# Expert stage: down projection of the odd experts as three products of split operands, five steps behind

## The reference

```
h = jnp.einsum('th,ehd->etd', xn, w1) + b1[:, None, :]
a = jnp.minimum(h[..., ::2], LIMIT)
b = jnp.clip(h[..., 1::2], -LIMIT, LIMIT)
s = a * jax.nn.sigmoid(ALPHA * a) * (b + 1.0)
y = jnp.einsum('eti,eih->eth', s, w2) + b2[:, None, :]
t = jnp.einsum('eth,te->th', y, gate_full)
return x + t.reshape(shape)
```

## Time and profile before

| | us |
|---|---|
| median of three runs | 1690.46 (1688.75, 1690.46, 1696.88) |
| the profiled execution | 1688.07 |
| its span, first to last instruction | 1686.30 |
| expert stage, first to last product of TensorE | 260.9 to about 867 |
| TensorE busy in the whole span | 1355.0 |
| VectorE busy in the whole span | 1255.6 |
| ScalarE busy in the whole span | 802.1 |

### The profile page before, as it was taken

One profiled execution on the slowest core, in us unless ns is written; L12 is line 12 of the kernel. 1 busy time (PEld: TensorE's weight loads), 2 busy tenths in 40 slices (PEclk: granted clock), 3 DMA queues, 4 the chain that ended last, 5 costly groups with the idle time before them and its releaser, 6 DMA issues. The chain is left out here.

```text
span 1686.3 us, 36641 instructions
## 1 busy us (share of the span) xinstructions
PE 1355.0 (80%) x13255; PEld 956.7 (57%) x13255; DVE 1255.6 (74%) x2799; ACT 802.1 (48%) x1432; POOL 145.7 (9%) x72
## 2 busy tenths in 40 slices
PE   0569998999999999999968888633777767678876
PEld 0456775666666666666636666432444544466665
DVE  6785127777777777777768999728888784799996
ACT  0564326666666666666646555311212211566663
POOL 2000000000000000000002443410000000112221
PEclk9879999999999999999989999867999999788887
DMA  8000003433334334333312433460223000111110
GB/s 226 1 0 0 6 5 103 116 114 114 113 113 112 108 113 113 113 113 114 113 42 75 125 112 126 129 236 24 78 106 124 31 29 32 54 57 56 56 56 19
DMA packets 122258, 142.22 MB, mean 84 GB/s; under 512 B 8768, under 2 KB 78752, under 8 KB 121120
## 3 DMA queue, kind: packets, MB, share of 16 engines
q1 hardware_dynamic: 118704, 134.81, 26.0%
q10 hardware_dynamic: 3440, 5.79, 1.0%
HBM read 106.49 MB, written 34.08 MB: 83 GB/s over the span
## 5 line engine op out<-in xcount | busy, mean ns | idle before, releaser
L919 ACT ACTIVATE glu_a<-moe_a,b1s 128x512 f32<-128x512 f32 x256 | 176.2, 688 | 227.8 <-PE moe_a L848 227.8
L865 PE MATMUL moe_y<-glu_a,w2s 128*128 128x512 f32 x512 | 261.3, 592 | 0.3 <-DVE glu_a L966 0.2
L949 DVE TENSOR_SCALAR b_raw<-b_raw 128x512 f32<-128x512 f32 x256 | 109.4, 427 | 146.9 <-ACT b_raw L924 146.6
L846 PE MATMUL moe_a<-x_hi,w_hi 128*128 128x512 f32 x256 | 192.5, 752 | 5.4 <-DVE w_lo L975 5.4
L924 ACT ACTIVATE b_raw<-moe_b,b1s 128x512 f32<-128x512 f32 x256 | 176.0, 687 | 2.6 <-PE moe_b L848 0.9
L966 DVE TENSOR_TENSOR glu_a<-glu_a,gate_row 128x512 f32<-128x512 f32 x256 | 175.8, 687 | 0.0
L958 DVE SCALAR_TENSOR_TENSOR glu_a<-glu_a,b_raw 128x512 f32<-128x512 f32 x256 | 175.6, 686 | 0.1
L865 PEld LDWEIGHTS moe_y<-glu_a,w2s 128*128 128x128 f32 x512 | 96.2, 188 | 23.9 <-DVE glu_a L966 2.0
L848 PE MATMUL moe_b<-x_hi,w_lo 128*128 128x512 f32 x256 | 101.9, 398 | 0.0
L848 PE MATMUL moe_a<-x_hi,w_lo 128*128 128x512 f32 x256 | 101.9, 398 | 0.0
L846 PE MATMUL moe_b<-x_hi,w_hi 128*128 128x512 f32 x256 | 101.9, 398 | 0.0
(11 more groups left out here) (252 smaller groups left out, 2791.8 us busy)
## 6 DMA issues: line engine op xcount, KB each, us to landing
gate_row<-gate_scratch SPq DMA_DIRECT2D x256, 256.0 KB, 3.1
kq_scratch<-kq_out SPq DMA_DIRECT2D x32, 256.0 KB, 3.5
kq_in<-kq_scratch SPq DMA_DIRECT2D x8, 1024.0 KB, 7.1
acc<-in_L_attn_inputs SPq DMA_DIRECT2D x8, 512.0 KB, 10.0
xq_scratch<-qT SPq DMA_DIRECT2D x16, 256.0 KB, 2.0
v_scratch<-v_out SPq DMA_DIRECT2D x16, 256.0 KB, 2.3
k_scratch<-k_out SPq DMA_DIRECT2D x16, 256.0 KB, 2.8
k_rows_scratch<-k_rows SPq DMA_DIRECT2D x16, 256.0 KB, 3.2
```

The source lines that it names most:

```text
L846: pe.matmul(bank[:, :], w1_hi[:, e, s, :], hi, start=True, stop=False)
L865: pe.matmul(bank, w["w2"][:, e, :], glu_a[e % 4][:, :], start=(e == 0), stop=(e == E - 1), skip_group_check=True).then_inc(down, 1)
L919: act.activation(glu_a[e % 4][:, :], ps_a[u][:, :], ACT.Gelu_apprx_sigmoid, bias=w["b1"][:, 0, e:e + 1]).then_inc(a_glu, 1)
L949: dve.tensor_scalar(b_raw[u][:, :], b_raw[u][:, :], 1.0 + LIMIT, 1.0 - LIMIT, ALU.min, ALU.max).then_inc(b_cut, 1)
```

## The change

For the eight odd experts, the fp32 down product is replaced by three one-pass products of split operands: w2 high x activation high, w2 high x activation low, w2 low x activation high. Four buffers of 128x512 hold the parts of the activation (`a_hi`, `a_lo`, two of each), two of 128x8x128 those of w2. The parts of w2 are made in the first tile, beside those of w1. The parts of the activation are made in even steps, of the weighed expert three steps back: the high one by ScalarE (a copy to fp32r, ahead of the gelu), the low one by VectorE (a subtraction, behind `multiply`). The odd experts' down products are five steps behind their up projection, in even steps; the even experts' stay one fp32 product, three steps behind, in odd steps. At the end the order is 11, 14, 13, 15. The gelu of an odd expert, which overwrites `glu_a`, waits for the low part of the expert four before it where it waited for that expert's product. `copy_y` waits for both counts.

```diff
--- before.py
+++ after.py
@@ -790,12 +790,23 @@
         ps_a = [ctx.enter_context(nc.psum_tensor(f"moe_a{i}", [P, TILE], F32)) for i in range(2)]
         ps_b = [ctx.enter_context(nc.psum_tensor(f"moe_b{i}", [P, TILE], F32)) for i in range(2)]
         ps_y = [ctx.enter_context(nc.psum_tensor(f"moe_y{i}", [P, SUBS, DIM], F32)) for i in range(2)]
+
+        w2_hi, w2_lo = sb("w2_hi", [P, EXPERTS // 2, DIM], F32R), sb("w2_lo", [P, EXPERTS // 2, DIM], F32R)
+        a_hi, a_lo = [sb(f"a_hi{i}", [P, TILE], F32R) for i in range(2)], [sb(f"a_lo{i}", [P, TILE], F32R) for i in range(2)]
+        w2_hi_ready, w2_lo_ready = sem("w2_hi_ready"), sem("w2_lo_ready")
+        a_hi_ready, a_lo_ready = sem("a_hi_ready"), sem("a_lo_ready")
+        down_split = sem("down_split")
         up_a, up_b, biased = sem("up_a"), sem("up_b"), sem("biased")
         b_copied, b_cut, a_glu = sem("b_copied"), sem("b_cut"), sem("a_glu")
         multiplied, weighted, down, added = sem("multiplied"), sem("weighted"), sem("down"), sem("moe_added")
         counted = sem("moe_counted")
         acc = w["acc"]
         E = EXPERTS
+        HALF = E // 2
+
+        def even_of(t, e):
+
+            return t * HALF + e // 2
 
         def before(t, e, k):
 
@@ -858,12 +869,23 @@
 
                 def down_proj(t, parity, e):
 
-                    pe.wait_ge(weighted, t * E + e + 1)
-                    if e == 0 and not (isinstance(t, int) and t < 2):
-                        pe.wait_ge(added, t - 1)
                     bank = ps_y[parity].rearrange("p j d -> p (j d)")
-                    pe.matmul(bank, w["w2"][:, e, :], glu_a[e % 4][:, :], start=(e == 0), stop=(e == E - 1),
-                              skip_group_check=True).then_inc(down, 1)
+                    if e % 2 == 0:
+                        pe.wait_ge(weighted, t * E + e + 1)
+                        if e == 0 and not (isinstance(t, int) and t < 2):
+                            pe.wait_ge(added, t - 1)
+                        pe.matmul(bank, w["w2"][:, e, :], glu_a[e % 4][:, :], start=(e == 0), stop=False,
+                                  skip_group_check=True).then_inc(down, 1)
+                        return
+                    i = e // 2
+                    if isinstance(t, int) and t == 0:
+                        pe.wait_ge(w2_lo_ready, i + 1)
+                    pe.wait_ge(a_lo_ready, even_of(t, e) + 1)
+                    hi, lo = a_hi[i % 2][:, :], a_lo[i % 2][:, :]
+                    pe.matmul(bank, w2_hi[:, i, :], hi, start=False, stop=False, skip_group_check=True)
+                    pe.matmul(bank, w2_hi[:, i, :], lo, start=False, stop=False, skip_group_check=True)
+                    pe.matmul(bank, w2_lo[:, i, :], hi, start=False, stop=(e == E - 1),
+                              skip_group_check=True).then_inc(down_split, 1)
 
                 def bias(t, parity):
 
@@ -880,16 +902,17 @@
 
                 def step(t, parity, e, more):
                     up(t, parity, e)
-                    if before(t, e, 3):
-                        tile, expert = before(t, e, 3)
-                        down_proj(tile, parity if e >= 3 else 1 - parity, expert)
+                    lag = 3 if e % 2 else 5
+                    if before(t, e, lag):
+                        tile, expert = before(t, e, lag)
+                        down_proj(tile, parity if e >= lag else 1 - parity, expert)
                     if e == 6 and not (isinstance(t, int) and t == 0):
                         turn_y(t - 1, 1 - parity)
                     if e == 9:
                         bias(t, parity)
 
                 def tail():
-                    for e in range(E - 3, E):
+                    for e in (E - 5, E - 2, E - 3, E - 1):
                         down_proj(TILES - 1, 1, e)
                     turn_y(TILES - 1, 1)
 
@@ -899,6 +922,16 @@
             def _(act):
                 def split(e):
                     act.activation(w1_hi[:, e, :, :], w["w1"][:, e, :, :], ACT.Copy).then_inc(w1_hi_ready, 1)
+                    if e % 2:
+                        act.activation(w2_hi[:, e // 2, :], w["w2"][:, e, :], ACT.Copy).then_inc(w2_hi_ready, 1)
+
+                def split_a(t, e):
+
+                    i, n = e // 2, even_of(t, e)
+                    act.wait_ge(weighted, t * E + e + 1)
+                    if before(t, e, 4):
+                        act.wait_ge(down_split, n - 1)
+                    act.activation(a_hi[i % 2][:, :], glu_a[e % 4][:, :], ACT.Copy).then_inc(a_hi_ready, 1)
 
                 def split_tile(t, parity):
                     if not (isinstance(t, int) and t < 2):
@@ -913,9 +946,14 @@
                         split(e + 2)
                     if e == 9 and more:
                         split_tile(t + 1, 1 - parity)
+                    if e % 2 == 0 and before(t, e, 3):
+                        split_a(*before(t, e, 3))
                     act.wait_ge(up_a, n + 1)
                     if before(t, e, 4):
-                        act.wait_ge(down, n - 3)
+                        if e % 2 == 0:
+                            act.wait_ge(down, even_of(t, e) - 1)
+                        else:
+                            act.wait_ge(a_lo_ready, even_of(t, e) - 1)
                     act.activation(glu_a[e % 4][:, :], ps_a[u][:, :], ACT.Gelu_apprx_sigmoid,
                                    bias=w["b1"][:, 0, e:e + 1]).then_inc(a_glu, 1)
                     act.wait_ge(up_b, n + 1)
@@ -927,13 +965,16 @@
                         copy_y(t - 1, 1 - parity)
 
                 def copy_y(t, parity):
-                    act.wait_ge(down, (t + 1) * E)
+                    act.wait_ge(down, (t + 1) * HALF)
+                    act.wait_ge(down_split, (t + 1) * HALF)
                     if not (isinstance(t, int) and t == 0):
                         act.wait_ge(y_turned, t)
                     act.activation(yT[:, :], ps_y[parity][:, :, :].rearrange("p j d -> p (j d)"), ACT.Copy)\
                        .then_inc(y_copied, 1)
 
                 def tail():
+                    split_a(TILES - 1, E - 3)
+                    split_a(TILES - 1, E - 1)
                     copy_y(TILES - 1, 1)
 
                 split_tile(0, 0)
@@ -974,6 +1015,19 @@
                     dve.wait_ge(w1_hi_ready, e + 1)
                     dve.tensor_tensor(w1_lo[:, e, :, :], w["w1"][:, e, :, :], w1_hi[:, e, :, :], ALU.subtract)\
                        .then_inc(w1_lo_ready, 1)
+                    if e % 2:
+                        dve.wait_ge(w2_hi_ready, e // 2 + 1)
+                        dve.tensor_tensor(w2_lo[:, e // 2, :], w["w2"][:, e, :], w2_hi[:, e // 2, :], ALU.subtract)\
+                           .then_inc(w2_lo_ready, 1)
+
+                def split_a(t, e):
+
+                    i, n = e // 2, even_of(t, e)
+                    dve.wait_ge(a_hi_ready, n + 1)
+                    if before(t, e, 4):
+                        dve.wait_ge(down_split, n - 1)
+                    dve.tensor_tensor(a_lo[i % 2][:, :], glu_a[e % 4][:, :], a_hi[i % 2][:, :], ALU.subtract)\
+                       .then_inc(a_lo_ready, 1)
 
                 def split_tile(t, parity):
                     if not (isinstance(t, int) and t < 2):
```

## The result

The changed kernel takes 1671.39 us (median of four, 1667.55 to 1673.22) against 1689.67 for the kernel before: ratio 0.988, interval 0.9847 to 0.9912. Five more executions of it, on one chip, gave 1672.67 against 1692.12, ratio 0.9882 (0.986 to 0.9904). The forecast was 1671, the range 1665 to 1682. The total was met; the sum behind it was not, and two misses cancelled in part. To see that, the span is cut in two: the expert stage (from the first up product to ScalarE's first instruction of the projection stage) and all the rest.

A forecast was written before the change was run, and what follows sets the result against it. TensorE, busy 50 of 50 us at full clock, was taken to bound the expert stage. Terms -20.6 + 0.4 + 1.2 = -19.0 us took 1688.07 to 1669.1, carried to a median of 1671 us; range 1665 to 1682.

The forecast's parts named there:

- the sum: Whole kernel: TensorE -20.6, first tile +0.4, tail +1.2, together -19.0 us.
- TensorE's gain: Expert stage: three one-pass products (0.696 us) replace an fp32 product (0.854), 0.158 us per odd expert, 20.6 us (18.3 to 21.4).
- rival D: Expert stage on TensorE: the skill pages' 0.216 us a product holds, gain 27 - 1.6 us, time 1665; chance 0.03.
- ScalarE: covered: Even steps: the extra 0.622 us copy fits ScalarE's 0.86 us wait before the gelu and costs nothing.
- VectorE: not the bound: Tiles 1 to 15: with the extra subtraction VectorE needs 32.2 us a tile against TensorE's 36.37, cost nothing.
- First tile: First tile, where VectorE also splits w1 and w2: 0.4 us of TensorE stall, bounds 0 and 2.0.
- Tail: End of the expert stage, last weigh to copy of y: net +1.2 us, bounds 0.8 and 1.6.
- Rival B: Expert stage: new waits in a ring set the pace, 4.8 us per pair, +40 us, 1730 us; chance 0.05.
- Outside the stage: All stages but the expert stage: untouched by the change, so a term of 0 in the sum.
- 2 us put on for the median: Total: the three runs' median lay 2.4 us above the profiled execution, so 1669.1 was raised to 1671.
- the ring of waits: Expert stage: odd gelu waits for VectorE's low part, that for ScalarE's high part, that behind the earlier b copy; 4.8 us per pair.

The follow-up runs named there:

- the cover used up: Changed kernel with ScalarE's copy made twice in each even step, the first into an unread buffer: tile period 36.139 us, expert stage 587.0 us.
- two subtractions: Changed kernel with VectorE's subtraction made twice in each even step, the first into an unread buffer: mean tile period 37.59 us, expert stage 612.3 us.
- three quarters split: Changed kernel with experts 2, 6, 10, 14 of tiles 1 to 15 also as three split products, seven steps behind: 1656.05 us against 1692.41, ratio 0.9785.

## Why the prediction was right, point by point

- **TensorE's gain: right in kind, its size too small.** The step that failed is "three one-pass products cost 0.696 us, so each odd expert saves 0.158 us". It is 0.187, above the upper bound of 0.164. Means over 100 plain steps of each kind in the changed kernel, from one L858 product of `moe_a` to the next, show where the missing 0.029 us lie. The triple takes 0.229 + 0.227 + 0.228 = 0.685 us and not 0.696. The six up products of its step take 1.385 and not 6 x 0.232 = 1.392. The step is thus 2.069 us, 0.177 less than the 2.246 of before. The other step of the pair, whose fp32 product stayed, takes 2.237, which is 0.009 less; the sum had that at nothing. 0.232 was the mean of five products of which two (L847, the low part of x as the moving operand) took 0.225 to 0.229 and three 0.233 to 0.235; the triple was costed by that mean, and it was taken for granted that neighbours keep their price. They don't: in the changed kernel the first five up products behind a triple take 0.227 to 0.228 us each, those behind an fp32 product 0.230 to 0.235 but for the first, which can't be read. Why was not tested. Fifteen periods make 22.4 us; at 0.158 for an expert they would have made 19.0.
- **The 0.216 us a product of rival D.** The Trainium skill ("TensorE: Matmul & The Clock Gate", Back-to-back issue gap) gives this price for products without neighbours, and about 0.131 for a sustained stream of weight loads and products. The saving estimated from 0.216 misses the measured 0.187 by as much as the forecast's 0.158 does. As a price the trace disagrees with it, before and after: no product of the stage took under 0.223 us from start to start.
- **ScalarE: covered.** Right, and more so than argued: the period stayed 36.139 us with the cover used up.
- **VectorE: not the bound.** Right. Its starts are 0.60 apart when it is full, and each instruction lasts 0.68. The Trainium skill ("VectorE: DVE Perf Modes", The DRAIN you can't avoid) has the next operation wait until the pipe is empty; in the trace it starts before the record of the one in front ends. The room is small: one more subtraction per pair and VectorE sets the pace, by 0.11 us a tile and the pauses at the loop's jumps.
- **First tile: stall under-estimated.** TensorE's weight loads in it (the 0.24 us of idle time before a load in an fp32 product's neighbourhood are usual, as in the earlier trace rows):

```profile
273.51 0.30 PEld L877 LDWEIGHTS moe_y<-glu_a,w2s 128*128 128x128 f32 x2 [0.48 <-DVE glu_a L1007]
...
278.07 0.30 PEld L877 LDWEIGHTS moe_y<-glu_a,w2s 128*128 128x128 f32 x2 [0.43 <-DVE glu_a L1007]
...
282.62 0.30 PEld L877 LDWEIGHTS moe_y<-glu_a,w2s 128*128 128x128 f32 x2 [0.41 <-DVE glu_a L1007]
```

  From the first down product to the first bias product are 14.12 us, 14.44 before. The products between them are 3 x 0.86 fewer and 2 x 0.685 more, 1.21 us less, so 0.9 us are stall (forecast 0.4, bounds 0 and 2.0). Without the subtraction 0.4 of it are left. From the bias product on the period is 36.14 at once. Against that, the way from the first up product to the first down product took 7.05 us in this trace, 7.83 before and 7.82 in the second trace of the changed kernel. It depends on when the granted clock rises to its upper level: seven products into the stage in this trace, eleven in the other two, at 0.427 us for each product ahead of that. So 0.8 of the 22.8 us are no gain of the change, by these two traces.
- **Tail: right.** The triple's chain, to be read beside the earlier trace rows:

```profile
841.56 0.69 DVE L1007 TENSOR_TENSOR glu_a<-glu_a,gate_row 128x512 f32<-128x512 f32 x1
...
842.29 0.63 ACT L934 ACTIVATE a_hi<-glu_a 128x512 fp32r<-128x512 f32 x1 [1.90 <-DVE glu_a L1007]
...
843.70 0.19 PEld L885 LDWEIGHTS moe_y<-a_hi,w_hi 128*128 128x128 f32 x1 [0.26 <-DVE a_lo L1029]
...
844.75 0.60 ACT L972 ACTIVATE yT<-moe_y 128x512 f32<-128x512 f32 x1 [1.83 <-PE moe_y L887]
```

  From the last weigh to the copy of y are 844.75 - 841.56 = 3.19 us against 866.01 - 864.10 = 1.91, 1.3 more; from the start of the last L857 product (L846 before) to the next stage 9.9 against 8.7. The forecast was 1.2.
- **Rival B** did not occur in the changed kernel: gelus waited 6.1 us for low parts in all, and none of it was seen by TensorE. With two subtractions they waited 163.5 us, and a tile without a jump took no longer than VectorE's own sum.
- **Outside the stage: zero is not shown to be right, and the first table's +5.7 is mostly the draw of its traces.** Four traces with the old order of TensorE's work had 1077.8, 1077.9, 1072.2 and 1077.9 us there. Those with the new order had 1082.6 to 1086.4 in seven and 1088.9 in the one with two subtractions, but the one with three quarters split, which changes the order further, had 1077.0. The timings leave 2.4 us (0.2 to 4.7). Of the 5.7 us between the first two traces, 1.6 lie ahead of the stage and 4.1 behind it: 7.0 more in the delta stage, hundreds of us behind the change, and 2.9 less in the others. A window of 140 us in its scan, kernel before, then the changed one (columns as in the earlier trace rows):

```profile
1160.00:1300.00 140.00, 99.35 (x4068) 66.89 (x4069) 114.74 (x390) 29.37 (x82) 0.00 (x0) 0.94 0.21 76
```

```profile
1138.00:1278.00 140.00, 103.14 (x3879) 68.83 (x3879) 109.90 (x363) 28.80 (x79) 0.00 (x0) 0.85 0.20 71
```

  The instructions are the same, the granted clock is 0.94 in one and 0.85 in the other, and fewer get done at 0.85. From its first product to the next stage the delta stage took 320.6 and 327.6 us, 324.6 in the second trace of the kernel before (0.89), and 320.2 with three quarters split (0.88). So the clock goes with it in part; what sets the clock there was not found. The traces with the buffers, the semaphores and ScalarE's and VectorE's extra instructions alone show no sign of it, but chance is not ruled out: single runs of the kernel before differ by up to 11.8 us, and so why there are 2.4 us, if there are, stays open.

So the sum's -19.0 stands against -22.7 in the stage and +2.4 in the rest by all timings, -20.3 together. That 1671 meets 1671.39 to 0.4 us is in part luck: a gain mis-sized by 3.7 us, a term outside the stage that was put at nothing, and 2 us put on for the median, where single runs scatter by 10 us. A mechanism that is right and a total that fits don't make the terms right: only the cut at the stage's ends showed the misses.

## What to carry to other kernels

Where TensorE is full and one-pass products of split operands are possible, the gain is (fp32 product - three products) for each one replaced, measured here at 0.187 us for 128x128 by 128x512, until the engines that make the parts are full; count their room by starts in a busy stretch, not by durations. Where a mean period is longer than that count, print the periods one by one before naming a cause: here the excess lay in every other tile, at the loop's jump back, and not in the ring of waits that the totals of waiting pointed to. A moved or late instruction costs nothing as long as its reader asks for it steps later: test the cover by using it up, before pricing its loss. Compare stages between traces, not only spans: scatter elsewhere is as large as a term of the sum, and what lies outside a stage is better taken from many timings than from one trace of each kernel.

## What the hardware showed that was not expected

- VectorE beside GpSimd: the one waits for the other to finish. `cut_b` takes 0.41 us or up to 1.5, 0.68 in the mean; `multiply` 0.68 or up to 1.8, 0.80 in the mean; the same subtraction takes 1.3 to 1.8 us on GpSimd, or 3.2 to 5.9.
- At the loop's jump back VectorE pauses 2.8 to 3.6 us in the two kernels with the longest and fullest loop on it, and 0.2 us in all others.
- One-pass products of 128x512 in one stream take from 0.225 to 0.235 us in the mean by their place in the order; with three quarters split most take 0.226 or 0.227.
- ScalarE's copies of 128x512 that last 0.62 us start 0.53 apart when none waits.
